# A pipelined tokenizer, attention and mixture layer: own distances in steps for the first and last three groups, and queries and keys stacked in runs of 8832 bytes

## The chip, the core and the metric

One core of one Trainium2 chip runs the whole program in one launch. The metric is the device time in microseconds of that core. The program before took 655.1 us, the median of three runs (655.05 to 660.72).

## The reference

Three layers over 128 clips of 90 channels and 750 samples, all in float32:

```python
h = patches(x) @ W.T + b              # (128, 46, 192): 46 patches of 16 samples x 90 channels a clip
y = layernorm(h)
q, k, v = y @ Wq, y @ Wk, y @ Wv
h = h + softmax(causal(q @ k.T)) @ v  # one head of 192
z = layernorm(h)
p = softmax(z @ W_gate.T + b_gate)    # 8 experts, the two largest kept
qkv = z @ W_qkv.T + b_qkv + 2 * sum_n p[n] * ((z @ A[n].T) @ B_lora[n].T)
out = multihead(qkv, heads=12)        # head dimension 16, over the 46 patches
h = h + out @ W_proj.T + b_proj
```

## The kernel before

The 128 clips go in 16 groups of 8. A group has 368 tokens (8 clips of 46), seen as 3 tiles of 128 tokens (the last two overlap) or as 4 pairs of clips of 92 tokens. Products that need float32 precision are made of float16 parts, a high part and a low one (`x = high + low`), each product as three or five matmuls: ScalarE (ACT) writes the high part, VectorE (DVE) or GpSimd (POOL) the low one.

Each engine has a hand-written list of operations for one step, and runs `step(s)` for s = 0, 1, ... An operation `op(n)` in step s works on group `s - LAG[op][n]`, if that group exists (`group`, L315); so each engine passes through all groups with a fixed distance between its operations. Engines wait for each other by semaphores only. All DMAs are issued by SyncE (SP), in the order of its own list. What the names mean, in the order of a group's life:

- `load_next(half)` on SP brings x of the next group into `raw`, half by half (L442). `high(n)` on ACT and `low(n)` on POOL (L641) split it in 8 and 16 pieces, 12 of 16 samples of a patch into `xs`, the other 4 into `xe`; `extra_rows` on SP copies `xe` into rows 96 and up of `xs` (L501).
- `tok(0..11)` on PE: the patch product, four parts for each tile of tokens, 108 matmuls a group, in one PSUM bank `ps_tok`; `h_tile`, `stats1` on DVE, `ln1` on POOL, `xn_tile`, `xn_twin` on ACT: first layer norm. `h_to_pairs` on SP copies h to pairs of clips (6 DMAs, L515).
- `xt` (transposes), `g` (x times Wq Wk^T), `v`, `sc` (scores), `max1`, `exp1`, `pt`, `av`, `h2`: first attention. `stats2`, `ln2`, `xn2`, `yt`: second layer norm.
- `ga` (gate and low-rank input), `logits`, `ranks`, `dispatch` on DVE, `ad` on POOL, `at`: router. `qk(0..2)`, `cv(0..1)`: queries, keys, values.
- `qk_to_scratch` writes queries and keys to DRAM (`w_in`), `stack_qk` reads them back as `q3` and `k3`: 16 dimensions of a head on partitions, three times, high, low and high (L538, L539). `place_v2` does the same for the values within SBUF (4 DMAs, L551).
- `s(p)` (24 small score products), `max2`, `shift`, `exp2`, `p` (transposes), `p2t` high and low, `pv`, `norm2`: second attention, pair by pair p = 0..3, with one buffer for scores `ps_s` and one for transposed weights `ps_p`.
- `ot`, `pr`, `fin`, `h2b` (h plus bias, on POOL), `store`: projection and output.

Every other product on PE takes the next of three rotating PSUM banks `ps_r`; `RING_AT` says which, and `bank_free` makes PE wait until the operation that had the bank last has been evacuated (`FREED`). Weights are transposed on PE in units (`unit`, `unit_high` on ACT, `unit_low` on DVE): those of the patch product ahead of the steps, the others by `weights(n)` inside the first steps, n = 0, 1, 2, each right behind an operation of group 0 (`WEIGHTS_AFTER`); `weights(2)` on DVE also makes biases and clears `p2T`, `v2` and `q3`. Their staging room is the room of `q3`, `k3` and `v2`. `middle_weights` and `late_weights` on SP load them, one behind each half of x of group 1.

The order of PE's list before is `p(3) g(0) tok(9) g(1) tok(10) pv(3) at tok(11) weights(0) s(0) ot(0) sc ot(1) s(1) qk(0..2) p(0) pt cv(0) av(0) av(1) weights(1) s(2) pr(0) xt(0) tok(0..3) pv(0) p(1) cv(1) s(3) xt(1) yt(0) tok(4) tok(5) pr(1) yt(1) tok(6) p(2) pv(1) tok(7) ga weights(2) v(0) v(1) tok(8) pv(2)`. `s` of a group comes 4 steps after its `tok`, `pr` 5 steps.

## Time and profile before

| | |
|---|---|
| median of three runs | 655.1 us |
| the profiled execution | 658.63 us |
| its span, first to last instruction | 656.9 us |
| mean granted TensorE clock | 0.943 of full |
| PE busy | 586.3 us (89%), 7805 matmuls |
| weight loads of PE busy | 523.9 us (80%) |
| DVE, ACT, POOL busy | 483.5, 355.6, 381.8 us |
| DMA queue of SP | 75057 packets, 81.63 MB, 61.2% of 16 engines |

PE is matmul, PEld the weight loads of TensorE, DVE is VectorE, ACT ScalarE, POOL GpSimd, SP SyncE. Engines count as busy from the start of an instruction to its end; matmuls overlap, so a busy PE is not PE at its peak. "L641" is line 641 of the kernel.

### The profile page before, as it was taken

How to read it: one execution, taken by the hardware profiler on the slowest of the kernel's cores; microseconds unless marked ns; L12 is line 12 of the kernel's file. 1: busy time of each engine (PE TensorE's matmuls, PEld its weight loads, DVE VectorE, ACT ScalarE, POOL GpSimd, SP SyncE). 2: the span in 40 equal slices, each digit the busy share in tenths (PEclk: the TensorE clock that was granted, in tenths of full speed). 3: DMA queues.
4: the chain of work that ended last, by engine and by line, in shares of the span. 5: the costliest groups of instructions: out<-in, count | busy, mean ns of one | idle time of the engine just before them, and what ended most of it. 6: DMA issues, size and time to landing. Idle time of an engine off the chain costs nothing.

```text
span 656.9 us, 20488 instructions
## 1 busy us (share of the span) xinstructions
PE 586.3 (89%) x7805; PEld 523.9 (80%) x7805; DVE 483.5 (74%) x1306; ACT 355.6 (54%) x688; POOL 381.8 (58%) x650
## 2 busy tenths in 40 slices
PE   3827798979999999999999999999999999887783
PEld 3726586869898989898989898989898897775673
DVE  5302457675888888888888888888887888986672
ACT  3434454655666666656666666565655545533331
POOL 6687646785767677676767676757575614121010
PEclk9977789998999999999999999999999999996876
DMA  8795622976494949594959595958584434461610
GB/s 201 162 181 124 152 66 63 164 183 102 124 159 136 160 133 162 136 168 137 155 147 168 139 159 143 161 144 154 150 153 90 77 69 70 72 95 30 106 35 19
DMA packets 75154, 82.94 MB, mean 126 GB/s; under 512 B 10137, under 2 KB 60645, under 8 KB 75057
## 3 DMA queue, kind: packets, MB, share of 16 engines
q1 hardware_dynamic: 75057, 81.63, 61.2%
q8 instruction: 62, 1.02, 0.8%
q14 instruction: 35, 0.29, 0.2%
HBM read 50.24 MB, written 13.57 MB: 97 GB/s over the span
## 4 chain that ended last, share of the span: by engine, by line
PE 74%; POOL 7%; DVE 6%; issue 6%; DMA 3%; ACT 2%; SPq 1%; POOLq 0%; ACTq 0%; DVEq 0%
PE ps_r L1324 23%; PE ps_tok L1316 6%; PE ps_tok L1317 6%; PE ps_tok L1318 6%; PE ps_p L1565 5%; POOL xs L641 4%; PE ps_s L1553 4%; PE ps_r L1316 4%; PE ps_r L1318 4%; PE ps_r L1317 4%; DMA raw<-x 3%; PE ps_r L1467 3%; PE ps_r L1595 2%; PE ps_r L1404 2%; PE ps_r L1480 2%
## 5 line engine op out<-in xcount | busy, mean ns | idle before, releaser
L641 POOL TENSOR_TENSOR xs<-raw,xs 90x368 f16<-90x368 f32 x192 | 163.9, 883 | 16.4 <-ACT xs L735 16.4
L1316 PE MATMUL ps_tok<-w_tok,xs 128*128 128x192 f16 x576 | 145.8, 253 | 2.9 <-issue 1.7
L1317 PE MATMUL ps_tok<-w_tok,xs 128*128 128x192 f16 x576 | 145.6, 253 | 0.0
L1318 PE MATMUL ps_tok<-w_tok,xs 128*128 128x192 f16 x576 | 145.4, 252 | 0.0
L649 POOL TENSOR_TENSOR ad<-ga,disp 128x384 f32<-128x384 f32 x16 | 13.4, 840 | 108.1 <-DVE disp L1151 108.1
L735 ACT ACTIVATE p2T<-ps_p 128x552 f16<-128x552 f32 x64 | 40.3, 630 | 65.7 <-PE ps_p L1565 53.8
L735 ACT ACTIVATE xs<-raw 90x736 f16<-90x736 f32 x96 | 75.5, 805 | 0.0
L1316 PEld LDWEIGHTS ps_tok<-w_tok,xs 128*128 128x128 f16 x576 | 66.8, 116 | 5.8 <-issue 1.9
L1317 PEld LDWEIGHTS ps_tok<-w_tok,xs 128*128 128x128 f16 x576 | 66.8, 116 | 1.7
L1318 PEld LDWEIGHTS ps_tok<-w_tok,xs 128*128 128x128 f16 x576 | 66.7, 116 | 0.3
L641 POOL TENSOR_TENSOR xe<-raw,xe 90x368 f16<-90x368 f32 x64 | 55.7, 883 | 17.8 <-ACT xe L735 17.8
L1316 PE MATMUL ps_r<-v,p2T 128*128 128x68 f16 x384 | 45.6, 200 | 12.5 <-DVE p2T L1069 11.1
L1565 PE MATMUL ps_p<-ident,p 110*128 110x110 f32 x384 | 49.4, 266 | 1.6 <-DVE p2T L1069 0.9
L1316 PEld LDWEIGHTS ps_r<-v,p2T 128*128 128x128 f16 x384 | 38.1, 100 | 15.8 <-DVE p2T L1069 12.6
L1084 DVE TENSOR_TENSOR o<-ps_r,rc 46x192 f32<-46x192 f32 x128 | 45.5, 355 | 4.2
L1069 DVE TENSOR_TENSOR p2T<-ps_p,p2T 128x552 f16<-128x552 f32 x64 | 46.3, 723 | 2.6 <-ACT p2T L735 1.6
L1061 DVE TENSOR_TENSOR df<-ps_s,mx 128x552 f32<-128x552 f32 x64 | 46.2, 723 | 1.2 <-issue 0.5
L1324 PE MATMUL ps_r<-x2T,w_qk 128*128 128x368 f16 x240 | 47.0, 328 | 0.0
L1318 PE MATMUL ps_r<-v,p2T 128*128 128x68 f16 x384 | 45.7, 199 | 1.4 <-issue 1.4
L1053 DVE TENSOR_REDUCE mx<-ps_s 128x12 f32<-128x552 f32 x64 | 46.2, 722 | 0.7 <-PE ps_s L1553 0.6
L1317 PE MATMUL ps_r<-v,p2T 128*128 128x68 f16 x384 | 45.7, 198 | 0.2 <-issue 0.2
L619 POOL TENSOR_TENSOR rs<-ve,minus_half 128x1 f32<-128x1 f32 (+1 forms) x64 | 42.7, 668 | 5.0
(175 smaller groups left out, 1566.5 us busy)
## 6 DMA issues: line engine op xcount, KB each, us to landing
raw<-x SPq DMA_DIRECT2D x32, 1035.0 KB, 8.3
qk_scratch<-qk SPq DMA_DIRECT2D x32, 276.0 KB, 3.0
q<-qk_scratch SPq DMA_DIRECT2D x48, 138.0 KB, 7.1
k<-qk_scratch SPq DMA_DIRECT2D x48, 138.0 KB, 7.7
xs<-xe SPq DMA_DIRECT2D x30, 184.0 KB
v<-v2s SPq DMA_DIRECT2D x64, 73.3 KB
out<-h2b SPq DMA_DIRECT2D x16, 276.0 KB
xs<-xe SPq DMA_DIRECT2D x15, 149.5 KB
```

The costliest lines, as they stand in the source:

```text
L619: nc.gpsimd.tensor_tensor(dst, ve, minus_half[0:rows, 0:cols], ALU.pow).then_inc(done, 1)
L641: nc.gpsimd.tensor_tensor(lo, src, hi, ALU.subtract).then_inc(s_lo, 1)
L735: return nc.scalar.activation(out_, in_, ACT.Copy, scale=scale)
L1053: nc.vector.tensor_reduce(mx[:].rearrange("p (a h) -> p a h", a=2), scores2(), AX_X, ALU.max).then_inc(s_mx, 1)
L1061: nc.vector.tensor_tensor(df[:].rearrange("p (a h) k -> p a h k", a=2), scores2(), mx[:].rearrange("p (a h) -> p a h", a=2).unsqueeze(3).t ...
L1069: nc.vector.tensor_tensor(p2T_used(1), ps_p_used(), p2T_used(0), ALU.subtract).then_inc(s_p2T, 1)
L1084: nc.vector.tensor_tensor(o2[r, p, 0:D].rearrange("p (h e) -> p h e", h=HEADS), pv[r, b, :, 0:HD], rc[r, p, :].unsqueeze(2).to_broadcast([ ...
L1316: mm(dst, stat[0], mov[0], start=start, stop=False)
L1317: mm(dst, stat[0], mov[1], start=False, stop=False)
L1318: return mm(dst, stat[1], mov[0], start=False, stop=stop)
L1324: last = mm(dst, stat(a), mov(b), start=start and n == 0, stop=stop and n == 4)
L1565: last = nc.tensor.transpose(ps_p[:, half, 128 * a:128 * a + ROWS], p2[0:ROWS, 6 * half + 2 * a:6 * half + 2 * a + 2, :].rearrange("p a b ...
```

## The change

1. Steps. `STEPS` goes from 24 to 32, all of `LAG` is new, and a table `MOVED` beside it gives, for groups 0, 1, 2 and 13, 14, 15 and each operation, by how many steps it is done earlier (first three) or later (last three) than `LAG` says. `group` asks `step_of`. For example `tok(0)` of groups 0, 1, 2, 3 now comes in steps 3, 5, 7, 10, `s(0)` of groups 0 to 2 in steps 11, 12, 13, and `pr(0)` of groups 13, 14, 15 in steps 26, 29, 31. The pipeline stays as deep: `s` four steps after `tok`, `pr` five.
2. Orders. The lists of all five engines and `RING_AT` are new. PE's list is now `sc at weights(4) weights(3) weights(2) tok(10) tok(11) pv(3) s(0) qk(0..2) pt weights(0) s(1) cv(0) av(0) av(1) p(0) tok(0) ot(0) tok(1) tok(2) ot(1) cv(1) tok(3) s(2) xt(0) p(1) tok(4) pv(0) pr(0) s(3) tok(5) pr(1) yt(0) yt(1) p(2) xt(1) tok(6) tok(7) pv(1) weights(1) ga g(0) g(1) v(0) p(3) tok(8) pv(2) v(1) tok(9)`.
3. Weights. They come in five portions with steps of their own. On PE: 0 and 1 in step 4 (after `tok` of group 0), 2 in step 5 (before `tok` of group 1), 3 in step 6, 4 in step 7 (before `tok` of group 2). The middle weights are loaded behind both halves of x of group 1, B_lora (`late_weights`) in SP's step 6, before `h_to_pairs` of group 0 and x of group 3.
4. Layout. The columns of queries and keys are ordered by dimension, then head (`by_dim`), so a partition of `q3` or `k3` takes one run of 12 x 368 values, 8832 bytes, instead of twelve runs of 736 bytes. The pad of `q3` is one of 36 columns at its end instead of one behind each head. The bias of queries and keys is loaded as one row, reordered and turned by three one-column matmuls instead of loaded as three columns.

Products, their shapes and all other DMAs are the same. The core of the diff:

```diff
-WEIGHTS = (range(M_FROM, GA_FROM), range(GA_FROM, PR_FROM), range(PR_FROM, ALL))
+WEIGHTS = [range(a, b) for a, b in ((M_FROM, GA_FROM), (GA_FROM, PR_FROM), (PR_FROM, PR_FROM + 4), (PR_FROM + 4, LORA_FROM),
+                                    (LORA_FROM, ALL))]
...
+LAG = {"store": (12,), "place_v2": (10,), "lateload": (6,), "load_next": (5, 5), "extra_rows": (6,),
+    "qk_to_scratch": (9,), "h_to_pairs": (7,), "stack_qk": (9,),
...
+MOVED = {"store": ((0, 0, 0, 3, 3, 3),), "place_v2": ((0, 0, 0, 0, 0, 3),),
+    "load_next": ((4, 4, 4, 0, 0, 0), (4, 4, 3, 0, 0, 0)), "extra_rows": ((4, 4, 0, 0, 0, 0),),
...
+def step_of(op, n, g):
+    at = g + LAG[op][n]
+    if op in MOVED and g < 3:
+        return at - MOVED[op][n][g]
+    if op in MOVED and g >= GROUPS - 3:
+        return at + MOVED[op][n][g - GROUPS + 6]
+    return at
...
-            g = s - LAG[op][n]
-            return g if 0 <= g < GROUPS else None
+            for g in range(GROUPS):
+                if step_of(op, n, g) == s:
+                    return g
+            return None
...
-        q3 = sb("q3", [128, HEADS, TG + PAD], F16)
-        k3 = sb("k3", [128, HEADS, TG], F16)
+        q3 = sb("q3", [128, HEADS * TG + PAD], F16)
+        k3 = sb("k3", [128, HEADS * TG], F16)
...
-        w_out = scratch.rearrange("a b (h d) n -> a b d h n", d=HD)
+        w_out = scratch.rearrange("a b (d h) n -> a b d (h n)", d=HD)
...
+        def by_dim(ap):
+            return ap.rearrange("p (d w) -> p w d", d=HD)
...
-                    if g is not None and g + 1 < GROUPS:
-                        sp.wait_ge(s_lo, g * 16 + (8, 16)[half])
-                        load_x(clips(g + 1, half), half)
-                        if g == 0:
-                            (middle_weights, late_weights)[half]()
+                    if g is not None and g > 0:
+                        sp.wait_ge(s_lo, g * 16 - (8, 0)[half])
+                        load_x(clips(g, half), half)
+                        if g == 1 and half == 1:
+                            middle_weights()
...
-                            sp.dma_start(q3[half + HD * n:half + HD * (n + 1), :, 0:TG], w_out[g % 2, qp, :, 0:HEADS, :]).then_inc(s_qk3, 16)
-                            sp.dma_start(k3[half + HD * n:half + HD * (n + 1), :, :], w_out[g % 2, kp, :, HEADS:2 * HEADS, :]).then_inc(s_qk3, 16)
+                            at = half + HD * n
+                            sp.dma_start(q3[at:at + HD, 0:HEADS * TG], w_out[g % 2, qp, :, 0:HEADS * TG]).then_inc(s_qk3, 16)
+                            sp.dma_start(k3[at:at + HD, :], w_out[g % 2, kp, :, HEADS * TG:2 * HEADS * TG]).then_inc(s_qk3, 16)
...
-                qk_to_scratch()
-                load_next(1)
-                stack_qk()
-                h_to_pairs()
-                store()
-                load_next(0)
-                place_v2()
-                extra_rows()
+                store()
+                place_v2()
+                late_weights()
+                load_next(0)
+                extra_rows()
+                qk_to_scratch()
+                load_next(1)
+                h_to_pairs()
+                stack_qk()
```

On DVE `weights(4)`, with the clearing of the rooms, now comes ahead of `h_tile(0)` of group 2, and `logits g_low(0) ranks dispatch g_low(1) norm2(2) stats1(0)` end its list; `p2t(3) max1 ad_low norm2(3)` begin it. On POOL `h2b` of groups 0 and 1 comes a step earlier than `LAG` says. In the last two groups DVE's order is, for group 15, `max2(0) shift(0) max2(1) shift(1) p2t(0) o_low(0) o_low(1) max2(2) shift(2) norm2(0) p2t(1) max2(3) shift(3) p2t(2) fin(0) fin(1) norm2(1) p2t(3) norm2(2) norm2(3)`, where `o_low` and `fin` are group 14's; before it was `max2(0) shift(0) o_low(0) o_low(1) max2(1) shift(1) p2t(0) max2(2) shift(2) norm2(0) fin(0) max2(3) p2t(1) fin(1) shift(3) norm2(1) p2t(2) norm2(2) p2t(3) norm2(3)`.

## Rows read from the trace of the kernel before

**Rows 1.** Windows: stretch, length, busy by engine (count), clock, DMA share, GB/s.

```profile
34.30:54.10 19.80, 3.43 (x27) 3.05 (x27) 2.46 (x8) 5.90 (x11) 15.51 (x27) 0.64 0.90 176
54.10:81.70 27.60, 23.63 (x203) 19.64 (x202) 10.34 (x37) 12.62 (x24) 20.35 (x36) 0.81 0.58 134
81.70:116.60 34.90, 30.82 (x282) 26.17 (x280) 21.40 (x65) 17.41 (x38) 17.95 (x30) 0.91 0.29 73
...
132.70:170.10 37.40, 33.82 (x452) 30.56 (x451) 26.62 (x75) 20.22 (x39) 24.26 (x42) 0.91 0.69 140
170.10:203.50 33.40, 33.37 (x481) 30.55 (x479) 28.48 (x80) 21.31 (x42) 23.33 (x40) 1.00 0.72 149
...
539.70:568.40 28.70, 25.45 (x372) 21.44 (x371) 26.29 (x73) 15.32 (x32) 8.81 (x19) 1.00 0.44 76
568.40:598.10 29.70, 22.68 (x338) 18.96 (x337) 24.94 (x65) 11.69 (x23) 8.35 (x12) 0.97 0.40 73
598.10:623.90 25.80, 21.30 (x279) 16.80 (x279) 16.72 (x33) 9.14 (x17) 0.06 (x1) 0.76 0.42 73
623.90:656.90 33.00, 19.82 (x249) 17.39 (x248) 17.39 (x35) 7.47 (x14) 1.83 (x1) 0.66 0.09 27
```

**Rows 2.** Chain that ended last, one piece met again: start, us, what.

```profile
161.00 2.54 PE ps_r L1324 x35
...
194.42 2.54 PE ps_r L1324 x35
```

**Rows 3.** Timeline of PE, end of `tok` of group 15: start us, us, what.

```profile
538.87 0.25 PE L1316 MATMUL ps_tok<-w_tok,xs 128*128 128x192 f16 x1
...
539.53 0.25 PE L1318 MATMUL ps_tok<-w_tok,xs 128*128 128x192 f16 x1
```

**Rows 4.** Timeline of the SP queue in the fill: start us, us, what.

```profile
24.55 0.53 SPq L442 DMA_DIRECT2D raw<-x  x1
...
30.58 11.22 SPq L434 DMA_DIRECT2D k<-L_ffn_B_lora  x6
...
43.91 2.27 SPq L501 DMA_DIRECT2D xs<-xe  x3
```

**Rows 5.** Chain that ended last, from 20 to 55 us: start, us, what.

```profile
30.10 11.00 DMA raw<-x
```

**Rows 6.** Timeline of POOL, last lows of group 0.

```profile
22.23 5.07 POOL L641 TENSOR_TENSOR xs<-raw,xs 90x368 f16<-90x368 f32 x6
```

**Rows 7.** Waits of PE, 21 to 133 us: us in total, times, longest.

```profile
PE ps_r L1404 <- ACT xn L910: 19.9, 3, 16.4
```

**Rows 8.** Timeline of PE, weight units of `weights(1)` and `weights(2)`.

```profile
73.75 0.80 PE L1346 MATMUL ps_s<-ident,q 128*128 128x128 f32 x3
...
78.99 0.58 PE L1344 MATMUL ps_p<-ident,k 96*64 96x96 f32 x2
...
90.81 0.41 PE L1346 MATMUL ps_s<-ident,q 96*128 96x96 f32 x3
...
93.37 0.67 PE L1346 MATMUL ps_s<-ident,k 96*128 96x96 f32 x3
...
96.32 1.01 PE L1324 MATMUL ps_s<-w_pr,o2T 128*92 128x192 f16 x5
```

**Rows 9.** Timeline of DVE, clearing of `v2`.

```profile
99.16 2.78 DVE L1020 MEMSET v<- 128x3264 f32 x1 [0.63 <-issue]
```

**Rows 10.** Chain that ended last, from 132 to 150 us.

```profile
140.72 1.86 POOL h2b L699
```

**Rows 11.** DMA issues: what, queue, kind, count, KB each, median us to landing.

```profile
q<-qk_scratch SPq DMA_DIRECT2D x48, 138.0 KB, 7.1
k<-qk_scratch SPq DMA_DIRECT2D x48, 138.0 KB, 7.7
```

**Rows 12.** Waits of PE, 540 to 660 us, the longest.

```profile
PE ps_r L1316 <- DVE p2T L1069: 11.1, 7, 3.1
```

More of the change, by code:

```diff
@@ L68 @@
-STEPS = 24
-RING_AT = {"g0": 1, "g1": 0, "pv3": 2, "at": 1, "ot0": 0, "sc": 2, "ot1": 1, "qk0": 0, "qk1": 2, "qk2": 1, "pt": 0,
-           "cv0": 2, "av0": 1, "av1": 0, "pr0": 1, "xt0": 0, "pv0": 0, "cv1": 2, "xt1": 0, "yt0": 1, "pr1": 2,
-           "yt1": 1, "pv1": 2, "ga": 1, "v0": 0, "v1": 2, "pv2": 0}
-HIGH_AFTER = (3, 4, 5, 6, 8)
+LAG = {"store": (12,), "place_v2": (10,), "lateload": (6,), "load_next": (5, 5), "extra_rows": (6,),
+    "qk_to_scratch": (9,), "h_to_pairs": (7,), "stack_qk": (9,),
+    "low": (4, 4, 4, 4, 4, 4, 4, 5, 5, 5, 5, 5, 5, 5, 5, 5), "ad": (8,), "ln1": (6, 6, 6), "h2b": (9,), "ln2": (7,),
+    "xn2": (7,), "xn2_twin": (7,), "exp2": (9, 9, 10, 10), "x2_high": (8, 8), "wact": (3, 3, 4, 6, 7),
+    "xn_high": (6, 7), "high": (4, 4, 4, 4, 5, 5, 5, 5), "p2t_high": (9, 9, 10, 10), "ga_copy": (8,),
+    "g_high": (7, 7), "v_copy": (7, 7), "router_exp": (8,), "ad_high": (8,), "qk_high": (8, 8, 8), "exp1": (7,),
+    "p1t": (7,), "o2_twin": (10,), "xn_tile": (6, 6, 6), "cv_high": (8, 8), "o_high": (10, 10), "xn_twin": (6,),
+    "p2t_low": (9, 9, 9, 10), "max1": (7,), "ad_low": (8,), "norm2": (9, 9, 9, 10), "stats1": (5, 6, 6),
+    "max2": (9, 9, 9, 9), "wdve": (3, 3, 3, 5, 6), "shift": (9, 9, 9, 9), "qk_low": (8, 8, 8), "h_tile": (5, 5, 6),
+    "h2": (7, 7), "cv_low": (8, 8), "stats2": (7,), "o_low": (10, 10), "fin": (10, 10), "xn_low": (6, 6),
+    "x2_low": (7, 7), "logits": (7,), "g_low": (6, 6), "ranks": (7,), "dispatch": (7,), "sc": (9,), "at": (10,),
+    "wpe": (4, 4, 5, 6, 7), "tok": (7, 7, 7, 7, 7, 7, 7, 7, 7, 7, 8, 8), "pv": (11, 11, 11, 12),
+    "s": (11, 11, 11, 11), "qk": (10, 10, 10), "pt": (9,), "cv": (10, 10), "av": (9, 9), "p": (11, 11, 11, 11),
+    "ot": (12, 12), "xt": (8, 8), "pr": (12, 12), "yt": (9, 9), "ga": (9,), "g": (8, 8), "v": (8, 8)}
@@ L380, in audio_tower @@
                 ([(0, st_a), (NR, st_g)], NR + N_EXP, w_ga, WS, ()),
-                ([(DH * a, qkvv[:, a, :]) for a in range(4)], 2 * D, w_qk, QS, ()),
+                ([(DH * a, qkvv[:, a, :]) for a in range(4)], 2 * D, w_qk, QS, None),
                 ([(DH * a, prv[:, a, :]) for a in range(2)], D, w_pr, WS, ()),
@@ L726, in step @@
                 low(4)
+                low(5)
+                low(6)
             for s in range(STEPS):
@@ L1257, in step @@
                 p2t(3)
-                g_low(0)
-                g_low(1)
+                max1()
+                ad_low()
                 norm2(3)
-                ad_low()
+                stats1(1)
                 max2(0)
+                weights(3)
+                weights(4)
                 shift(0)
-                o_low(0)
-                max1()
-                o_low(1)
+                qk_low(0)
+                weights(0)
+                h_tile(2)
+                qk_low(1)
+                stats1(2)
+                qk_low(2)
                 max2(1)
-                stats1(1)
                 shift(1)
-                qk_low(0)
-                qk_low(1)
-                h_tile(2)
-                qk_low(2)
-                stats1(2)
-                weights(0)
-                p2t(0)
                 h2_(0)
+                cv_low(0)
                 h2_(1)
@@ L1286, in step @@
                 fin(0)
-                h_tile(0)
-                stats1(0)
-                cv_low(1)
+                xn_low(0)
+                weights(2)
+                p2t(1)
+                fin(1)
                 max2(3)
                 x2_low(0)
-                p2t(1)
-                fin(1)
+                x2_low(1)
+                shift(3)
                 xn_low(1)
-                shift(3)
-                x2_low(1)
                 norm2(1)
@@ L1300, in step @@
                 logits()
-                weights(2)
+                g_low(0)
                 ranks()
+                dispatch()
+                g_low(1)
                 norm2(2)
-                dispatch()
+                stats1(0)
             for s in range(STEPS):
@@ L1357, in value_bias @@
                 pe.wait_ge(s_bv, 5)
-                deep_product(unit_bank(ALL, PT_, D), lambda n: bias_v[:, n, :], lambda n: w_pr[:, n, :], True, True).then_inc(p_bv, 1)
+                deep_product(unit_bank(ALL, PT_, D), lambda n: bias_v[:, n, :], lambda n: w_pr[:, n, :], True, True)
+                for t in range(3):
+                    last = mm(unit_bank(ALL, 128, D + 3)[:, D + t:D + t + 1], b_dim[:, 128 * t:128 * (t + 1)], ident[0:1, 0:1],
+                              start=True, stop=True)
+                last.then_inc(p_bv, 1)
             for n in range(M_FROM):
```

215 lines of the change are left out of this document (119 added, 96 removed), and 21 rows, old and new, of tables (LAG, MOVED).

## The prediction, made before the changed kernel was run

> **What bounds the kernel now.** I read the share of each engine by stretch first, then the chain that ended last, then the timeline of PE and of the SP queue where PE stands idle. The stretches [rows 1] are cut at two kinds of mark: before 132.7 where the patch product (`tok`) of a new group begins, from 132.7 on where the second score product (`s`) of a new group begins. The reader is to see three regimes. From 170.1 to 539.7 PE is busy 33.37 of every 33.40 us at full clock, and the same piece of the chain returns after 194.42 - 161.00 = 33.42 us [rows 1, 2]: PE sets the pace, with DVE at 28.5 and POOL at 23.3 of 33.4. Before that the kernel fills: five groups enter in 170 us, and from 34.3 to 54.1 PE does 3.4 us of work. After 539.7 it drains for 117.2 us, in which PE is busy 89.3 us (25.45 + 22.68 + 21.30 + 19.82) and DVE 85.3; neither is full.
>
> The steady part is at its floor: in a patch product eight matmuls of 192 columns start within 539.53 - 538.87 = 0.66 us [rows 3], 82 ns apart, and 192 columns at the full clock of 2.4 GHz are 80 ns. So the change can win only at the ends, and could lose in the middle. The Trainium skill (Perfetto Trace Analysis, Identifying the Most-Contended Engine) says that matmul busy share is no measure of headroom and that the share of weight loads is to be read instead; by that reading PE would have slack in the middle. The starts 82 ns apart speak against it here.
>
> **The fill, part by part.** The sum goes from mark to mark.
>
> *To the first `tok` of group 1 (54.16 now).* Now SP issues the first half of x of group 1 at 24.55, then the middle weights, and the second half at 30.10; it lands 11.00 us later [rows 4, 5]. PE's next work, the transpose `xt` of group 0, waits 16.4 us for `xn` [rows 7], because POOL, in order, does the lows of group 1's second half before it finishes group 0's statistics. After the change both halves of x stand ahead of the middle weights. The second half waits for POOL's last low of group 0, 22.23 + 5.07 = 27.30 [rows 6], instead of going at 30.10. It no longer stands behind 0.65 MB of weights: now 1.7 MB (1.06 of x, 0.43 of W_qkv, 0.2 of smaller weights, by their shapes) land by 41.1; in the new order the 1.06 MB come first, at about 37.7, and the weights end at the same 41.1 or so. Extra rows of group 1 need POOL's tenth low, about 41.7 (eight lows from 33.1 on and two more, at 0.85 each, which is 5.07 / 6 [rows 6]); issuing takes 2.27 us [rows 4] and they queue behind the 1.06 MB of group 2's first half, so they land at about 48.5. Meanwhile PE, idle now, does weight units: `weights(1)` at 41.2, 5.8 us as now (73.75 to 79.57), then the four units of the new `weights(2)`, 2.6 us (90.81 to 93.37) [rows 8]. Then `tok` of group 1: 49.6, say 50 with the extra rows close behind. **Gain 4**, and 8.4 us of weight units lie in what was a hole. `xt` of group 0 now stands behind four parts of `tok` and does not wait.
>
> *To `tok` of group 2 (27.6 us now).* The 5.8 us of units go; the rest of the old `weights(2)`, 97.33 - 93.37 = 4.0 us [rows 8], comes in; of PE's 4.0 us of idle time here (27.6 - 23.6 [rows 1]) 1.9 go, since `xt` of group 1, one of the three waits of [rows 7], no longer stands at the head of the next step. 27.6 - 5.8 + 4.0 - 1.9 = 23.9, so 73.9. **Gain 3.7.** This takes for granted that group 2's extra rows are there. SP now issues six B_lora loads in 11.22 us [rows 4]; they move to about 48.5 to 59.7, then the six pair copies of h, x of group 3, and the extra rows at about 65 to 67; with 1.6 MB in the queue (they took 7 to 8 us above) they land at about 72.5. That is 1.4 us ahead of need, the thinnest place of the fill.
>
> *To `tok` of group 3 (34.9 us now).* The 6.5 us of units go, and the 4.1 us in which PE is idle (34.9 - 30.8 [rows 1]), which wait mostly for DVE: a memset of 2.78 us and two small ones stand ahead of the router steps [rows 9], so `ad` is late. What comes: one `cv` pair, 1.7 us, and a new stall. DVE's `weights(4)` (the memsets, some 3.7 us of which 2.78 [rows 9], and five short steps) now stands ahead of `h_tile(0)` of group 2, for which the second tile of `tok` waits: 5 us. 34.9 - 6.5 - 4.1 + 1.7 + 5 = 31.0, so 104.9. **Gain another 4.** The stall has a lower bound of 0 (hidden by late x) and an upper one of 8 with everything on DVE's list in series.
>
> *To the first `s` of group 0 (16.1 us now), PE full: 16.1.* So 121.0 against 132.7: of the three gains 11.7 stand.
>
> *To `s` of group 1 (37.4 now).* Full PE would need 33.4 less `ot` and `pr` of a group, 2.5: 30.9. Now 6.5 more: the chain runs through POOL's lows and the 1.86 us `h2b`, by which DVE, then `xt`, are late [rows 10], and the clock granted falls to 0.91 of full, which is the low level of 1.2 GHz for a part of the stretch [rows 1]. POOL has worked ahead by then in the new order, and `h2b` of group 0 stands one step earlier; I keep 2 of the 6.5: 32.9, so 153.9. **Gain 4.5.** Fill in all: 170.1 - 153.9 = 16.
>
> *Extra work.* Query and key columns written by dimension: evacuations of `w_qk` and of one `w_lora` unit become strided writes. Nearest is `weights(1)` as a whole, 5.8 us [rows 8], half of which at most hangs on them: free at best, half as long again at worst, 0 to 3 us, and in the hole; taken 0. Three one-column matmuls and a small copy replace three tiny loads: below 0.5.
>
> **The middle: 0.** Eleven steps of 33.42 and 2.0 us of odd stalls make the 369.6 us from 170.1 to 539.7; the amount of PE work does not change. I followed PE's three rotating banks through one new step. The tightest are `xt(1)`, which needs the bank that `fin(1)` frees, with only `yt`, `yt`, `p` (about 1.2 us) between; `cv(0)`, which needs `qk_low(1)`'s; and `sc`, which needs `g_low(1)`, now behind ranks and dispatch. I reckon 0.6 to 1.2 us to spare at these; they fit as long as DVE (28.5 of 33.4) keeps its phase.
>
> *The stacked runs.* q and k land 7.1 and 7.7 us after issue [rows 11] and the first `s` comes much later in both orders, so in the middle they are hidden behind other PE work. At the end the waits of PE after 540 that are worth a row go to DVE, none to a DMA [rows 12]. Uncovered they would cost at most 7.7 once at each end. Taken 0; the gain is bounded by 0 and 7.7.
>
> **The drain: 117.2 to 113.** The work is the same and as deep: `s` four steps behind `tok`, the projection five, before and after. PE waits 11.1 us in seven places for `p2T` from DVE [rows 12], which does attention's max, shift and low parts in the order written. The new order puts the shift and low part of the next pair ahead of outputs and norms in the last two groups, and `at` and `qk` of group 15 earlier. A third of the 11.1 is 4. Bounds: 0, and 117.2 - 85.3 - 5.5 (last output to end) = 26 were DVE full. Value near the low end, since each stage is a chain of one group through four engines. The clock falls to 0.76 and 0.66 in the last two stretches [rows 1], so the low level of 1.2 GHz filled 2 x 0.24 x 25.8 = 12 and 2 x 0.34 x 33.0 = 22 us of them; PE was busy in some 24 of these, full speed would halve that, and perhaps half of the 12 lies on the chain. I leave the clock as it is. The Trainium skill (Perfetto Trace Analysis, Matmul Optimizations) says the engine scales with utilization so that back-to-back matmuls keep it fast; were the new drain dense enough, the sum would be 6 us lower by it.
>
> **Sum.** 656.9 - 16 - 4 = 636.9 of span. The profiled execution took 658.63, 1.7 above its span and 3.5 above the median of 655.1; so against the median: 655.1 - 20 = 635.
>
> **Rivals.**
> *The fill is bound by x and POOL, not by the order (20%).* For it: DMA stood at 0.90 of its time from 34.3 to 54.1 and POOL at 15.5 of 19.8 [rows 1]; B_lora's 11 us of SP now stand in front of group 2's extra rows. Against it: DMA is at 0.58 and 0.29 afterwards. Then only the first 4 and half of the next gains stay: 655.1 - 4 - 2 - 2 = 647.
> *The middle slows (9%): slower than before.* One wait per step at one of the three tight banks, some 12 steps. From 20/12 = 1.7 us a step it eats the gain; at 2.3, 663. For it: in-order DVE with 4.9 us of slack a step. Against: the middle before runs without one such wait in 11 steps at the same load.
> *The middle quickens (2%).* If PE's own order hides gaps, the bound would be its weight loads, 30.55 of 33.40 [rows 1]: 2.85 us a step, 31 in 11 steps, 604. Against it are the starts 82 ns apart [rows 3]. (This is what the Trainium skill's rule named above would give.)
> *The stacked layout does nothing to the time* (likely, and counted in the main case): no term rests on it; alone it would give 655.
> *Main case (69%)*: 635, own range 626 to 645.
>
> **Chances and range.** Low end 624: below it 5% of the main case, the quickened middle, and a drain at half its bound. High end 652: above it the slowed middle and a little of the first rival. About 1% (648.5 to 661.7) is what a measurement of this kernel tells from no change. Faster: 69 + 2 + most of 20 minus a margin for both, 0.82; within 1%: 0.10; slower: 0.08.
>
> **What the new profile would show.** `tok` of group 1 near 50, of group 2 near 74, of group 3 near 105; first `s` near 121, the second near 154; weight transposes between 41 and 50; PE 33.4 of 33.4 in a step, period 33.42; some 113 us from the last group-12 `s` to the end; q and k landing in 4 to 7 us. Wrong would be: a period above 33.6; PE waiting for POOL's lows or extra rows after 70; more than 8 us of stall at `tok`'s second tile of group 2; a drain above 117.

## The result, and the profile after

The changed kernel is slower: 664.6 us median (659.6 to 671.6, 20 runs) beside 657.5 us (652.1 to 664.0, 20 runs) for the kernel before on the same chips; the ratio is 1.0104, 95% interval 1.008 to 1.0128. The forecast was 635.0 us, with a range of 624 to 652. Ratios, here and below, leave out executions more than 1.5% above their kernel's fastest, and medians are of all executions. The profiled execution took 671.6 us, 7 above its median, so what it loses in the middle is an upper value; what I read from it is where the time goes.

| us from mark to mark | before | forecast | after |
|---|---|---|---|
| start to first `s` of group 1 (fill) | 170.1 | 153.9 | 165.4 |
| eleven steps to first `s` of group 12 (middle) | 369.6 | 369.6 | 390.5 |
| from there to the end (drain) | 117.2 | 113 | 114.1 |
| span | 656.9 | 636.9 | 669.9 |

The drain came out as forecast, the fill gave 5 us instead of 16, and the middle, which was to stand still, lost 21. Its steps are no longer alike. Windows of the changed kernel (columns as in [rows 1]), three steps in a row and one later step, then fill and drain:

```profile
165.38:198.58 33.20, 33.20 (x482) 30.59 (x479) 29.11 (x80) 21.22 (x41) 21.77 (x39) 1.00 0.54 109
198.58:238.10 39.52, 36.22 (x483) 33.08 (x480) 29.43 (x80) 21.23 (x41) 23.52 (x40) 0.91 0.70 151
238.10:271.37 33.27, 33.27 (x483) 30.59 (x481) 29.17 (x79) 21.10 (x41) 23.49 (x40) 1.00 0.62 121
338.04:374.28 36.24, 33.40 (x486) 30.61 (x483) 29.37 (x80) 21.10 (x41) 23.50 (x40) 1.00 0.67 142
34.20:52.55 18.35, 12.96 (x64) 8.09 (x64) 7.48 (x12) 10.11 (x16) 15.71 (x27) 0.63 0.84 180
74.59:109.14 34.55, 27.49 (x265) 24.46 (x263) 22.19 (x65) 16.87 (x34) 24.46 (x42) 0.90 0.41 100
126.86:165.38 38.52, 33.25 (x452) 30.03 (x451) 26.31 (x72) 19.99 (x38) 23.25 (x39) 0.91 0.78 163
555.84:669.90 114.06, 86.98 (x1211) 72.96 (x1209) 84.20 (x203) 42.74 (x86) 17.69 (x32) 0.85 0.29 62
```

Every first step takes 33.2 us with PE full, a little better than the 33.42 of [rows 1, 2]. Every second one takes 36 to 39.5. Next stand PE's waits from 150 to 540 us (total, times, longest), and then one place of its timeline:

```profile
PE ps_tok L1380 <- issue: 16.6, 5, 3.6
```

```profile
206.39 0.73 PE L1634 MATMUL ps_p<-ident,p 110*128 110x110 f32 x6
210.42 0.32 PE L1380 MATMUL ps_tok<-w_tok,xs 128*128 128x192 f16 x1 [3.30 <-issue]
...
210.70 0.36 PE L1382 MATMUL ps_tok<-w_tok,xs 128*128 128x192 f16 x1
210.86 0.36 PE L1380 MATMUL ps_tok<-w_tok,xs 128*128 128x192 f16 x1
```

With one more at 140.3 in the fill there are six such waits (140.3, 210.4, 283.5, 354.6, 424.4, 496.2; 21.4 us), all before the first matmul of `tok`. "issue" means that the profile shows no releaser. In the code `tok(0)` waits there for three things: the `h` of the tile before, POOL's eighth low and the landing of its group's extra rows. The first two were long done at 210.4:

```profile
183.55 3.44 POOL L697 TENSOR_TENSOR xs<-raw,xs 90x368 f16<-90x368 f32 x4
202.26 0.35 DVE L1156 SCALAR_TENSOR_TENSOR h<-ps_tok,b_tok_bc 128x192 f32<-128x192 f32 x1
```

The eighth low ended at 186.99 and `h` at 202.61. So the landing of the rows is left, though the trace has no landing times for them; the runs below test it. The SP queue of two steps, with the stand of SP at the store:

```profile
214.16 0.42 SPq L594 DMA_DIRECT2D k<-qk_scratch  x1
224.99 0.28 SPq L613 DMA_DIRECT2D out<-h2b  x1
225.37 5.50 SPq L606 DMA_DIRECT2D v<-v2s  x4
230.91 1.24 SPq L496 DMA_DIRECT2D raw<-x  x1
232.26 4.02 SPq L555 DMA_DIRECT2D xs<-xe  x3
...
253.53 0.42 SPq L594 DMA_DIRECT2D k<-qk_scratch  x1
258.26 0.28 SPq L613 DMA_DIRECT2D out<-h2b  x1
258.64 9.82 SPq L606 DMA_DIRECT2D v<-v2s  x4
268.50 1.61 SPq L496 DMA_DIRECT2D raw<-x  x1
270.22 2.72 SPq L555 DMA_DIRECT2D xs<-xe  x3
```

```profile
SPq L613 <- DVE h2b L1313: 61.6, 10, 10.4
```

SP stands for the store's data (10.4 us, then 4.3), then spends 5.5 to 10.7 us issuing `place_v2`, and only then sends x's first half and the rows. Before, x went 12.7 us after the start of `tok` and 20.8 before the next one; now it goes 19 to 22 after and 14 to 16 before. (The half of x that goes here belongs to the group after; what it does to this `tok` is to go ahead of its rows.) `tok` starts at 210.42, 15.3 us after x (195.13) and 12.9 after the rows (197.52); x itself landed at 208.1. In the steps with a wait the rows had gone only 9.6 to 10.3 us ahead of the moment at which PE was ready for `tok`, in the steps without one 12.3 to 14.3. That gives the alternation: a wait makes its step long, the next rows come in time, and after a step of 33.2 us they don't. The low clock makes most of the long steps longer still, but it is not needed: the one of 36.24 us has its wait (2.84) and a clock of 1.00.

### The profile page after: what moved, and what is told of

Read it like the earlier page. It is cut to its first block, busy times and chain, and to the rows that moved or that the text cites. A ratio compares the mean times of both kernels' runs of the same rounds, so it can differ in the third digit from the quotient of the medians.

```text
span 669.9 us, 20517 instructions
## 1 busy us (share of the span) xinstructions
PE 592.8 (88%) x7811; PEld 530.6 (79%) x7811; DVE 497.3 (74%) x1307; ACT 355.9 (53%) x688; POOL 384.8 (57%) x650
## 4 chain that ended last, share of the span: by engine, by line
PE 77%; DVE 7%; issue 7%; POOL 4%; DMA 2%; ACT 1%; SPq 1%; DVEq 0%; POOLq 0%; ACTq 0%
PE ps_r L1388 24%; PE ps_tok L1380 7%; PE ps_tok L1382 7%; PE ps_tok L1381 7%; PE ps_p L1634 5%; PE ps_s L1621 4%; PE ps_r L1380 4%; PE ps_r L1382 4%; PE ps_r L1381 4%; PE ps_r L1535 3%; PE ps_r L1664 2%; POOL xs L697 2%; PE ps_r L1472 2%; PE ps_r L1548 1%; DMA b_row<-L_ffn_b_qkv 1%
## 5 line engine op out<-in xcount | busy, mean ns | idle before, releaser
L1380 PE MATMUL ps_tok<-w_tok,xs 128*128 128x192 f16 x576 | 149.1, 259 | 29.7 <-issue 21.4
L1381 PE MATMUL ps_tok<-w_tok,xs 128*128 128x192 f16 x576 | 148.6, 258 | 0.0
L1382 PE MATMUL ps_tok<-w_tok,xs 128*128 128x192 f16 x576 | 148.5, 258 | 0.0
L1380 PEld LDWEIGHTS ps_tok<-w_tok,xs 128*128 128x128 f16 x576 | 67.4, 117 | 33.2 <-issue 23.9
L1381 PEld LDWEIGHTS ps_tok<-w_tok,xs 128*128 128x128 f16 x576 | 67.7, 117 | 0.7
L1382 PEld LDWEIGHTS ps_tok<-w_tok,xs 128*128 128x128 f16 x576 | 67.6, 117 | 0.6
L918 ACT ACTIVATE qk<-ps_r,b_qk 128x368 f16<-128x368 f32 x48 | 27.2, 567 | 60.6 <-PE ps_r L1382 60.6
L1380 PE MATMUL ps_r<-v,p2T 128*128 128x68 f16 x384 | 45.5, 199 | 4.8 <-DVE p2T L1129 3.6
L791 ACT ACTIVATE xe<-raw 90x736 f16<-90x736 f32 x32 | 26.0, 812 | 41.5 <-DMA xs<-xe 32.2
L1634 PEld LDWEIGHTS ps_p<-ident,p 110*128 110x128 f32 x384 | 40.7, 145 | 9.1 <-issue 4.8
L1382 PE MATMUL ps_r<-v,p2T 128*128 128x68 f16 x384 | 45.5, 199 | 0.0
## 6 DMA issues: line engine op xcount, KB each, us to landing
raw<-x SPq DMA_DIRECT2D x32, 1035.0 KB, 11.9
```

What stands on the lines that cost most here:

```text
L791: return nc.scalar.activation(out_, in_, ACT.Copy, scale=scale)
L1380: mm(dst, stat[0], mov[0], start=start, stop=False)
L1381: mm(dst, stat[0], mov[1], start=False, stop=False)
L1382: return mm(dst, stat[1], mov[0], start=False, stop=stop)
L1634: last = nc.tensor.transpose(ps_p[:, half, 128 * a:128 * a + ROWS], p2[0:ROWS, 6 * half + 2 * a:6 * half + 2 * a + 2, :].rearrange("p a b ...
```

## The experiments

Theory 1: SP's order, the store and `place_v2` ahead of x and the rows, makes the rows late. Theory 2: the runs of 8832 bytes make the transfers around them late (x's median time to landing rose from 8.3 to 11.9 us).

| run | median us | ratio to before | 95% |
|---|---|---|---|
| store_behind | 698.0 | 1.063 | 1.059 to 1.068 |
| x_first | 704.7 | 1.076 | 1.071 to 1.081 |
| old_layout | 665.3 | 1.012 | 1.006 to 1.018 |
| layout_alone | 657.8 | 1.002 | 1.000 to 1.005 |
| store_x_place | 647.9 | 0.984 | 0.978 to 0.990 |
| store_x_place_rows | 662.3 | 0.999 | 0.994 to 1.004 |
| place_ahead_before | 654.5 | 0.997 | 0.994 to 1.001 |
| last_unmoved | 670.3 | 1.018 | 1.012 to 1.025 |
| rooms_behind | 647.3 | 0.985 | 0.980 to 0.990 |
| place_first_once | 647.4 | 0.986 | 0.981 to 0.991 |
| clean_last_unmoved | 649.6 | 0.988 | 0.984 to 0.993 |
| all_mended | 654.0 | 0.994 | 0.990 to 0.997 |
| store_from_act | 664.0 | 1.001 | 0.997 to 1.006 |
| place_from_act | 793.9 | 1.208 | 1.203 to 1.214 |
| store_act_x_first | 657.3 | 0.999 | 0.995 to 1.002 |
| v2s_doubled | 641.3 | 0.976 | 0.970 to 0.981 |
| v2s_doubled_mended | 641.6 | 0.975 | 0.970 to 0.979 |
| x_first_old_layout | 652.9 | 0.993 | 0.989 to 0.997 |

### The layout: old_layout and layout_alone

The changed kernel with the old runs of 736 bytes, and the kernel before with the new ones. The heart of the first edit:

```diff
-        w_out = scratch.rearrange("a b (d h) n -> a b d (h n)", d=HD)
+        w_out = scratch.rearrange("a b (h d) n -> a b d h n", d=HD)
...
-                            sp.dma_start(k3[at:at + HD, :], w_out[g % 2, kp, :, HEADS * TG:2 * HEADS * TG]).then_inc(s_qk3, 16)
+                            sp.dma_start(k3[at:at + HD, :, :], w_out[g % 2, kp, :, HEADS:2 * HEADS, :]).then_inc(s_qk3, 16)
```

> The changed kernel with queries and keys laid out as before (head, then dimension, runs of 736 bytes), the order kept. Theory 1 (order of the SP queue): PE still waits in front of tok in every second step, 15 to 25 us in all; ratio 1.00 to 1.02. Theory 2 (the long runs): x's first half lands in about 8.3 us again, no waits, ratio 0.970 to 0.98.

> The kernel before with the new layout alone (by dimension, then head, runs of 8832 bytes, the bias turned on PE), its order untouched. Theory 1: nothing that can be measured, 0.995 to 1.003, q and k landing in 5 to 6.5 us instead of 7.1 and 7.7. Theory 2: waits in front of tok as in the changed kernel, ratio above 1.02.

Both times are as theory 1 says. With the old layout the waits stay (same view and stretch as above), x still needs 11.7 us, and the order alone costs 1.2%:

```profile
PE ps_tok L1380 <- issue: 15.2, 7, 4.0
```

The layout alone is 1.0024 (1.0001 to 1.0046); `q` and `k` land in 6.8 and 7.4 us, not in the 5 to 6.5 that I expected. Theory 2 falls. But the two traces show a term that I had taken at 0. The same evacuation on ACT, in the changed kernel and then with the old layout:

```profile
43.86 1.93 ACT L791 ACTIVATE w_qk<-ps_p 128x384 f16<-128x384 f32 x1 [0.55 <-PE ps_p L1410]
```

```profile
42.76 0.49 ACT L791 ACTIVATE w_qk<-ps_p 128x384 f16<-128x384 f32 x1 [0.55 <-PE ps_p L1410]
```

Writing by dimension, with steps of 48 bytes, takes four times as long; on DVE it is 1.93 instead of 0.56. The first `tok` of group 1 starts at 50.4 instead of 52.6, 0.6 of which is an earlier landing of the weights. The Trainium skill (SBUF — State Buffer, Door 1: The DMA port swizzle) says that SBUF has lines of 16 bytes and that each access that crosses to a new one pays; with steps of 48 bytes every element does, and the longer row agrees with it. No run here separates that cause from others.

### The order on SP, first attempt: store_behind and x_first

```diff
-                store()
                 place_v2()
                 late_weights()
                 load_next(0)
                 extra_rows()
+                store()
```

In `x_first`, `place_v2()` moves behind `extra_rows()` as well.

> The changed kernel with one line moved: on the SP queue store() stands behind extra_rows() instead of at the head of the step. Theory 1 (SP stands at the store, up to 10.4 us, until DVE has written the last outputs, so x's first half and the extra rows leave some 9 us later against the patch product than before): both leave 5 to 8 us earlier, the waits of PE named issue in front of tok (six, 21.4 us) go or shrink below 5 us in all, and so does the low clock behind them; the step is 33.2 to 33.5 us on average; about 0.970 of the kernel before (range 0.963 to 0.98). Theory 2 (the runs of 8832 bytes make x and the extra rows land late): the waits stay, ratio 1.005 to 1.015.

> The changed kernel with place_v2() and store() both behind load_next(0) and extra_rows() on the SP queue. Theory 1: x's first half no longer stands behind the 5.5 to 9.9 us in which place_v2 is issued either; no wait before tok at all; equal to the run with the store alone behind if that has no waits left, otherwise faster by what it has left: 0.96 to 0.97. A rival to it: place_v2 now leaves later and the pv product or POOL's lows wait instead; then slower than the run with the store alone. Theory 2: the waits stay, 1.005 to 1.015.

x does go earlier and most of the waits before `tok` go, yet both runs are 5 to 6% slower than the changed kernel. The store was moved past its own deadline: POOL's `h2b` of group g writes into the buffer that the store of group g - 2 reads. Waits of POOL, then of PE, 150 to 540 us of `store_behind`:

```profile
POOL h2b L755 <- DMA out<-h2b: 73.3, 9, 11.2
```

```profile
PE ps_r L1664 <- DVE h L1247: 36.4, 9, 5.2
PE ps_tok L1380 <- issue: 3.4, 2, 2.2
```

DVE's `h2` waits for POOL, and PE's `ot` for the bank that `h2` reads. So with two buffers of `h2b` the store can't be moved back this far on SP; `place_v2` alone remains to be tried.

### The order on SP, mended: store_x_place, store_x_place_rows, place_ahead_before

```diff
                 store()
-                place_v2()
                 late_weights()
                 load_next(0)
                 extra_rows()
+                place_v2()
```

> The changed kernel with place_v2() behind load_next(0) and extra_rows() on the SP queue; store() stays at the head of the step, so that POOL's h2b doesn't wait for it (in the run with the store behind extra_rows it waited 7.26 us for it). Theory 1, mended (x's first half and the extra rows leave too late, because the store's wait and the 5.5 to 9.9 us of place_v2 both stand ahead of them): x's first half leaves 20 us or more ahead of the next tok instead of 15; no PE waits named issue before tok; step 33.2 to 33.5; ratio 0.97 to 0.98. Rival: place_v2, some 10 us later now, is what PE or POOL waits for next; then 1.0 or above.

0.984 (0.978 to 0.990): faster than both kernels, a little less than the 0.97 to 0.98 expected, and no wait before `tok` in the middle. The SP queue and a window over ten steps of this run:

```profile
184.09 0.28 SPq L613 DMA_DIRECT2D out<-h2b  x1
185.59 0.35 SPq L496 DMA_DIRECT2D raw<-x  x1
188.11 4.42 SPq L555 DMA_DIRECT2D xs<-xe  x3
192.64 7.90 SPq L606 DMA_DIRECT2D v<-v2s  x4
```

```profile
197.19:530.49 333.30, 332.45 (x4793) 305.98 (x4790) 290.44 (x791) 202.27 (x402) 225.46 (x380) 1.00 0.65 140
```

x goes 20.0 us and the rows 17.5 us ahead of the next `tok` (205.57). The step is 33.3 us.

> The changed kernel with the SP order of the kernel before at this place: store, load_next(0), place_v2, extra_rows. x's first half leaves early, the extra rows as late as in the changed kernel (some 13 us ahead of tok) but 10 us behind x instead of right behind it. If what makes tok wait is the megabyte of x that lands ahead of the rows: no waits, ratio 0.97 to 0.98, as with place_v2 behind both. If it is the time at which the rows themselves are issued: waits of 2 to 4 us in every second step as in the changed kernel, 1.00 to 1.01.

The rows' place counts too. Here x has 20.8 us but the rows, behind `place_v2`, only 9.9, and `tok` waits seven times in the profiled execution, 0.3 to 3.5 us (9.2 in all). The waits are smaller than in the changed kernel, but they stay: the ten times spread from 653.7 to 666.5, their median is 1.007 of that of the kernel before, and the profiled one is the shortest. So where `tok` waits, the rows took about 9 to 10 us from their issue with x well ahead of them (195.24 to 205.09), and about 13 right behind x in the changed kernel. My either-or was too narrow: both distances count.

> The kernel before with place_v2() moved ahead of load_next(0), the order that the changed kernel has. x's first half then leaves some 7 us later, 13 us ahead of the next tok instead of 20.8, the extra rows right behind it. Theory 1: tok waits for the rows in some steps, 1 to 4 us each, ratio 1.01 to 1.03. If place_v2's place is harmless and only the store's wait counts: 0.997 to 1.003.

0.997 (0.994 to 1.001): no loss, the second branch. x goes 15.6 us and the rows 12.8 ahead of `tok`, and `tok` waits once in the middle:

```profile
333.18:368.38 35.20, 33.54 (x480) 30.49 (x479) 28.50 (x80) 21.44 (x42) 23.31 (x40) 1.00 0.71 144
```

This fits a least distance of some 13 us for rows right behind x; it is no fixed number, since once in the changed kernel 12.3 was enough (387.80). It says too that `place_v2` ahead of x is harmless where it begins early: here 23 us ahead of the next `tok` and done after 7.5 (at 188 and 211.6), in the changed kernel 21 ahead (225.4 and 246.6) and at times 9.8 long. The swap alone is not the cause. The late begin, the long issue and the swap together are what differs, and taking the swap back is enough to end the waits (`store_x_place`).

### Which of the two: store_from_act, place_from_act, store_act_x_first

```diff
# store_from_act: the store leaves SP's list and stands in ACT's
                 p2t(2)
                 exp2(3)
+                store()
...
+                        nc.scalar.dma_start(out_v[:, g * PAIRS:(g + 1) * PAIRS, :], h2b[:, g % 2, :, :]).then_inc(s_out[g % 2], 16)
```

ACT's list reaches this place at the end of a step, so the store's `LAG` is 11 there instead of 12, and so in `store_act_x_first`; that of `place_v2` in the next run is 9 instead of 10.

> The changed kernel with the stores of the output issued from ACT, after exp2(3), instead of from SP; SP's order is otherwise that of the changed kernel (place_v2, x, rows). If SP's stand at the store (61.6 us in 10 steps) is what makes x and the rows late: both leave 5 to 10 us earlier, no waits named issue before tok, POOL doesn't wait for the store (as it did when the store was moved back on SP), 0.975 to 0.985. If it is the issuing of place_v2 (5.5 to 9.9 us): waits of 1 to 4 us stay in every second step, 1.0 to 1.01.

The second branch: 1.001, and 1.010 by the median of all ten executions, which spread from 654.2 to 671.6. With no store on SP `place_v2` begins earlier, but x gains little, since the same four copies now take longer to issue. Two steps of its SP queue:

```profile
213.03 0.42 SPq L594 DMA_DIRECT2D k<-qk_scratch  x1
216.43 8.13 SPq L606 DMA_DIRECT2D v<-v2s  x4
224.61 1.66 SPq L496 DMA_DIRECT2D raw<-x  x1
...
250.85 0.42 SPq L594 DMA_DIRECT2D k<-qk_scratch  x1
251.37 12.45 SPq L606 DMA_DIRECT2D v<-v2s  x4
263.86 3.30 SPq L496 DMA_DIRECT2D raw<-x  x1
```

12.45 us straight behind the loads of q and k, 8.13 after a pause of 3 us, 5.50 after one of 10.4 (first fence on SP). So the store's stand was in part free: much of the time that it took, the issuing would have taken. Four waits of `tok`, 2.3 to 4.4 us and 12.8 in all, stay in the middle between 200 and 530 us.

> The changed kernel with place_v2's four copies issued from ACT, after exp2(3), the store at the head of SP's step. If the issuing of place_v2 on SP is what makes x and the rows late: they leave right behind the store, 5.5 to 9.9 us earlier, no waits before tok, 0.975 to 0.985. If the store's wait alone does it: waits as in the changed kernel, 1.0 to 1.01. Cost of its own: ACT stands for as long as it issues (up to 10 us a step, with 21 of 33 us busy), which can make p2T or the exponentials late: up to 1.03.

1.208, far above the 1.03 given as its worst: x goes early, and ACT pays. Timeline of ACT in this run:

```profile
299.43 8.36 ACTq L983 DMA_DIRECT2D v<-v2s  x2
307.90 0.51 ACT L777 ACTIVATE ga<-ps_r 128x408 f32<-128x408 f32 x1 [8.83 <-issue]
```

Two of the four copies keep ACT for 8.4 us, and the router's `ga` waits behind them; PE waits 64.9 us for `ga` between 200 and 530 us. The Trainium skill (DMA: Bandwidth & Descriptors, Issuing engines are not separate DMA queues) says that starting DMAs from a second engine only saves the first one's time to start them, usually small beside the transfer. Here it is 5.5 to 12.5 us for four copies of 293 KB together, in a kernel where 1035 KB of x take some 7 to 15 us from issue to landing; how long the copies themselves take, the trace doesn't show.

> The stores issued from ACT and, on SP, x and the rows ahead of place_v2. If the two add: 0.970 to 0.98. If one of them already takes all waits before tok away, place_v2's lateness (v2s, 3.9 us once in the fill) makes this one the slower of the two: 0.98 to 0.99.

0.999, slower than `store_x_place`. No waits before `tok` in the middle, but seven of `ot` for `h` (7.3 us); ACT waits 30.2 us for `place_v2`'s copies to leave `v2s`. The rival of that expectation, and more of it than I gave.

### Back to the fill: rooms_behind, place_first_once, all_mended

On top of `store_x_place`: the three memsets behind `h_tile(0)`; `place_v2` of group 0 ahead of x; both with the old layout.

```diff
-                            clear_rooms()
...
                 h_tile(0)
+                if group(s, "wdve", 4) == 0:
+                    clear_rooms()
```

> The run with store, x, rows, place_v2 on SP (0.984), and on DVE the three memsets that clear the rooms stand behind h_tile(0) of group 2 instead of ahead of it. If the 6.15 us for which PE stands in front of tok's second tile of group 2 are DVE's memsets (v2's ends at 83.78, h follows at once, tok starts at 84.20; the page puts the wait down to POOL): the wait goes to 2.5 us or less, tok of group 3 starts at about 104 to 105 instead of 108.2, and 3 to 4 us of it reach the end if nothing else takes its place: 0.978 to 0.98. If it is POOL's lows: unchanged, 0.984.

The profile of the changed kernel puts the 6.1 us before `tok`'s second tile of group 2 down to POOL:

```profile
PE ps_tok L1380 <- POOL xs L697: 6.1, 1, 6.1
```

Its DVE timeline shows what was really late; the other fence is DVE in `rooms_behind`:

```profile
81.00 2.78 DVE L1080 MEMSET v<- 128x3264 f32 x1 [0.63 <-issue]
83.73 0.33 DVE L1156 SCALAR_TENSOR_TENSOR h<-ps_tok,b_tok_bc 128x192 f32<-128x192 f32 x1
```

```profile
79.23 0.34 DVE L1155 SCALAR_TENSOR_TENSOR h<-ps_tok,b_tok_bc 128x192 f32<-128x192 f32 x1
```

With `h` 4.5 us earlier the wait is below 2, and `tok` of group 3 starts at 105.1 instead of 108.2: DVE it was. But a wait of 3.0 for `xnT` takes part of it, the first `s` of group 1 gains 1.3, and the middle takes 372.4 us instead of 366.5: 0.985, no gain.

> The run with store, x, rows, place_v2 on SP (0.984), except that place_v2 of group 0 alone stays ahead of x. If the 3.9 us for which PE waits at 141.7 for v2s are the single buffer v2s, still being placed because its four copies are issued behind x and the rows (123.45 to 133.5): the wait goes, the first score product of group 1 comes at 160 to 161 instead of 164.0, ratio about 0.979, but x and the rows of the groups after leave later, so that up to 3 us may come back as a wait before tok. If it is something else: 0.984.

The wait for `v2s` goes and one of 4.3 us for the rows comes at 139.0: 0.986, nothing gained. It is the same exchange once more.

> Store, x, rows, place_v2 on SP, place_v2 of group 0 ahead of x, the memsets behind h_tile(0), and the old layout of queries and keys, whose evacuations take 0.5 us instead of 1.93. Each of the three adds what its place in the fill shows, if they don't hide one another: 6.1 - 2.5, 3.9 and 1.9 us, together some 9 of 643.6 us of span: ratio 0.968 to 0.975. If they overlap: 0.976 to 0.98.

Wrong: 0.994, slower than `rooms_behind` and `place_first_once` and as slow as its third part alone (`x_first_old_layout` below, 0.993). It meets 6.8 us of waiting for the rows at 137.4, and its middle takes 376.6 us against 366.5.

### The single buffer: v2s_doubled, v2s_doubled_mended, x_first_old_layout

```diff
-        v2s = sb("v2s", [PT_, 2, 2, PAIRS // 2, HEADS // 2, 2, HD + 1], F16)
+        v2s = sb("v2s", [PT_, 4, 2, PAIRS // 2, HEADS // 2, 2, HD + 1], F16)
...
-                        if g:
-                            act.wait_ge(s_v2, g * 64)
+                        if g > 1:
+                            act.wait_ge(s_v2, (g - 1) * 64)
```

> The run with store, x, rows, place_v2 on SP (0.984), and v2s in two buffers instead of one. If the late place_v2 is dear only because v2s has one buffer: ACT no longer waits for its copies (19.1 us in nine steps), PE's 3.9 us at 141.7 in the fill go, the first score product of group 1 comes at 160 to 161 instead of 164.0, the middle stays at 33.2 a step; 0.976 to 0.981. If not: 0.984.

0.976, the fastest together with the next; its interval (0.970 to 0.981) just meets that of `store_x_place` (0.978 to 0.990). In `store_x_place` ACT waits nine times for `place_v2`'s copies:

```profile
ACT v2s L791 <- DMA v<-v2s: 19.1, 9, 3.3
```

With two buffers that row is gone, and the eleven steps of the middle are full; window of this run:

```profile
163.90:528.94 365.04, 365.04 (x5260) 336.38 (x5260) 318.01 (x865) 227.81 (x443) 245.84 (x416) 1.00 0.67 142
528.94:642.00 113.06, 85.94 (x1212) 72.35 (x1209) 84.12 (x203) 42.72 (x86) 17.52 (x32) 0.87 0.30 62
```

The fill gains less than expected: the first `s` of group 1 comes at 162.4, not at 160 to 161, and stands 1.2 us before its second part at 163.9. The 3.9 us at `cv` are gone, so that this stage takes 33.3 us from the first `s` of group 0 to that of group 1 instead of 37.0, but the first `s` of group 0 comes 2 us later, behind the landing of k (2.3).

> The same with the memsets behind h_tile(0) and the old layout as well. If v2s was what gave the fill's gain back in the two mended runs (0.985 and 0.994), it now arrives: 0.965 to 0.972. If the middle stands against something else, as DVE's or SP's own phase: 0.975 to 0.99, with PE's waits at ot for h as there.

0.975: half right. The fill's gain now arrives (first `s` of group 1 at 157.1, with 1.7 us of waiting in it), and the span is 640.0; but medians show no difference from `v2s_doubled`. Its step over ten steps is 33.32 us (168.95 to 502.19) against 33.20 with the long runs, 1.2 us in ten steps.

> The run with store, x, rows, place_v2 on SP (0.984) with the old layout of queries and keys and nothing else. If the strided evacuations cost what the two disturbed profiles show (tok of group 1 at 50.4 instead of 52.5): 1.5 to 2.2 us less, 0.980 to 0.982. If they hide behind what comes next, or if the long runs are worth as much later: 0.984.

Wrong in sign: 0.993. The fill does gain, 4.3 us (first `s` of group 1 at 159.7), so the strided writes cost more than I read: they also stand on DVE ahead of the memsets (`w_lora`, 1.97 us instead of 0.68 for two). The middle then takes 377.6 us instead of 366.5, ACT waiting for `v2s` for 29.9 us in ten steps instead of 19.1 in nine; `k` lands in 7.8 us, `q` in 7.0 (7.3 and 6.3). How much of these 11 us belongs to the short runs is open. With two buffers they cost the ten steps 1.2 us, and in the changed kernel, with its waits for the rows, nothing (`old_layout`'s middle takes 390.1 us, the changed kernel's 390.5). And an earlier fill comes with a longer middle with the long runs too (`rooms_behind`).

### The drain: last_unmoved and clean_last_unmoved

```diff
-        if op in MOVED and g >= GROUPS - 3:
+        if False:
```

> The changed kernel with the last three groups at the same distances as the others (the table of shifts used for the first three alone). The middle and the fill are as in the changed kernel. If the table gives the drain its 3 us (114.1 us after 117.2 from the first score product of group 12 to the end): the drain takes 116 to 120 us, ratio 1.014 to 1.02. If the new base order gives them and the table nothing: 114 us, 1.005 to 1.015.

> The run with store, x, rows, place_v2 on SP (0.984, drain 113.1 us), with the last three groups at the same distances as the others. If the table of shifts gives the drain nothing (112.9 us without it, 114.06 with it, in the two profiles with a disturbed middle): 0.982 to 0.987, drain 112 to 114. If it gives what the ratios of those two suggested (1.018 against 1.010): 0.990 to 0.994, drain 116 to 119.

The drains take 112.9 and 112.4 us without the table's shifts for the last three groups, 114.1 and 113.1 with them. In the profiles they bring nothing; the 3 to 5 us against 117.2 come with the new base order. The ratios point the other way (1.018 against 1.010; 0.988 against 0.984), but within their intervals. In the second pair the traces have that difference in the middle (370.1 us against 366.5), in two steps of 35.8 and 35.3 us that end before 310 us, when no operation of the last three groups has been reached. Up to there the two programs do the same. So those 3.6 us are what one execution differs from another, and a difference of that size between two single traces, here and above, shows little by itself.

## Why the prediction was wrong, point by point

**"The middle: 0." This is the step that failed**, and it decides the sign. I followed PE's three banks through the new step and took the amount of PE work for the period. The bank reading holds: in `v2s_doubled` all three tight banks fit in eleven steps with PE full, and the step is 0.2 us shorter than before. What I didn't follow through the steady step was SP's list, though the diff prints it: `store`, `place_v2`, then x and rows, where before it was `store`, x, `place_v2`, rows. I had worked out just this wait for group 2 of the fill, as "the thinnest place", and there it did not come. It came one step of the reasoning further, in every second step from group 4 on. I also gave the rows 7 to 8 us from issue to landing; where `tok` waited for them it was about 13 right behind x, and 9 to 10 with x well ahead. What the runs put in place of the 0: five waits for the rows, 16.6 us, which with the clock that falls after most of them make the middle 20.9 us longer; with `place_v2` behind x and the rows they are gone and the middle takes 366.5 us, 3 less than before.

**The rival "the middle slows" (9%)** gave 663 from 2.3 us a step; measured are (390.5 - 369.6) / 11 = 1.9 us and 664.6. Its size a step was right, its mechanism (a PE bank) was not, and I left it outside the range. That the total fits as well is luck: 663 has the whole gain of 20 us in it, and the fill gave 5 where 16 were forecast. What I held against it, that the middle before runs without such a wait at the same load, says nothing about a list whose order is new.

**The fill, 16 forecast, 4.7 measured.** Term by term: `tok` of group 1 at 52.6 (50): the units take 11.6 us instead of 8.4, 1.9 us at a time in the strided evacuations that I had put at 0, with PE at the low clock for much of the stretch (0.63). `tok` of group 2 at 74.6 (73.9): right. `tok` of group 3 at 109.1 (104.9): the stall at the second tile came as forecast, 6.15 us for 5, by the memset ahead of `h_tile(0)`; the rest is the low clock in part of the stretch (0.90) and DVE's waits. First `s` at 126.9 (121.0). From there 38.5 us instead of 32.9: 4.9 of them the first of the waits for the rows, and the stretch has a clock of 0.91, as in [rows 1]. With that wait gone it is 37.0 (`store_x_place`), because 3.9 us of waiting for the single `v2s` took its place; with both gone it is 33.3 and 33.1 (`v2s_doubled`, `v2s_doubled_mended`). So the 4.5 us of gain which I gave this stage were there, behind two DMA deadlines that I hadn't followed.

**The drain, 113.** Measured 114.1, and 110.9 to 114.4 in every run with the new order but `place_from_act` (127.4). The size was right, the cause given was not: I took a third of PE's 11.1 us of waits for `p2T` off [rows 12]. They are all still there (530 to 680 us of the changed kernel):

```profile
PE ps_p L1634 <- DVE p2T L1129: 7.4, 5, 3.2
PE ps_r L1380 <- DVE p2T L1129: 3.6, 3, 1.9
```

**The layout.** "No term rests on it" held (1.0024 alone, and 1.012 for the changed kernel without it beside 1.010 with it). That it costs 2 to 4 us in the fill, a term that I took at 0 of a stated 0 to 3, and that it may give some of that back in the middle, I didn't see. q and k land in 6.2 and 6.9 us, within the forecast.

**The extra work.** "Below 0.5" was too low: turning the bias keeps PE for 0.82 us, with six matmuls instead of three, and DVE for another 0.88. What that adds to the time no run separates.

```profile
73.11 0.82 PE L1424 MATMUL ps_s<-ident,b_dim 1*128 1x1 f32 x6
```

`b_row`'s load is now the last of the middle weights to land (3.9 us of waiting at 40.9), at the time forecast for the weights, 41.1.

No run reached the 20 us. The best two runs have spans of 642.0 and 640.0, 15 and 17 below: fill 8 and 13, middle 3 and 0, drain 4 in both.

## What to carry to other kernels

When the order of a steady step changes, follow the DMA queue's own list through that step as carefully as the bounding engine's: for each transfer the distance from its issue to its reader, and what stands or issues ahead of it. A transfer moved away from one deadline has another behind it (the store's buffer, the staging buffer that a copy empties); find that one before moving it. Where two deadlines squeeze, a second buffer can take one of them away: here the order was worth 2.6% (1.010 to 0.984) and the buffer some 0.8% more. A wait that the profile calls "issue" in front of an instruction with a DMA semaphore is most likely that DMA, once the instruction's other releasers are seen to be long done.

## What the runs showed of the hardware

**A wait of PE costs more than itself when the clock falls after it.** The wait of 3.30 us makes its step 39.52 instead of 33.20 us, 6.3 longer; the clock of the stretch is 0.91 of full, and the matmuls of `tok` behind the wait start 160 ns apart instead of 82 [rows 3], which is the low level of 1.2 GHz. In two steps with a clock of 1.00 the wait cost little more than itself: one of 2.84 us in the changed kernel cost 3.0 (the row of 338.04), one of 1.63 in `place_ahead_before` 1.8 (the row of 333.18).

**Issuing is work.** In the lines above the same four copies of 73 KB each kept SP for 5.5 to 12.5 us, longest straight behind the loads of q and k, and ACT for 8.4 us for two of them. Why, the traces don't show.
